# A Q projection that comes out transposed, rotated along partitions, and raw weights loaded in place

## What is computed

```python
def apply_rope(x):                       # x: b, t, heads, 128
    phase = tile(pos[:, None] * inv_freq[None, :], (1, 2))
    return x * cos(phase) + rotate_half(x) * sin(phase)    # rotate_half: (-x2, x1)

q = apply_rope((layernorm(x) @ Wq).reshape(b, t, 32, 128))
k = apply_rope((ctx @ Wk).reshape(b, t, 8, 128));  v = (ctx @ Wv).reshape(b, t, 8, 128)
logits  = 30 * tanh(q k^T * 0.0884 / 30)               # 4 query heads share one of 8 K/V heads
weights = softmax(where(mask, logits, -1e30))
x = x + tanh(g_xattn) * (weights @ v).reshape(b, t, 4096) @ Wo
h = silu(layernorm(x) @ Wg) * (layernorm(x) @ Wu)      # Wg, Wu, Wd: 4-bit, dequantised, 512 x 1376
x = x + tanh(g_ffn) * (h @ Wd).astype(float16)
```

## Time and profile before

| | |
|---|---|
| median of three runs | 811.78 us |
| the profiled execution | 811.05 us, span 809.3 us |
| TensorE busy | 772.4 us, 95% of the span |
| VectorE, GpSimd, ScalarE busy | 616.4, 494.1, 352.7 us |
| mean granted TensorE clock | 0.982 |
| slots 8 to 60 | 9.12 us each, 100% TensorE |

### The profile page before, as it was taken

The page is one execution under the profiler, slowest core; times in us unless marked ns, Lnnn a source line. Parts: engine busy times, 40 slices in busy tenths (PEclk is TensorE's granted clock), DMA queues, the critical chain, the costliest instruction groups (busy, mean ns, idle before and its releaser), DMA issues.

```text
span 809.3 us, 12403 instructions
## 1 busy us (share of the span) xinstructions
PE 772.4 (95%) x3905; PEld 644.7 (80%) x3905; DVE 616.4 (76%) x1290; ACT 352.7 (44%) x715; POOL 494.1 (61%) x391
## 2 busy tenths in 40 slices
PE   4799999999999999999999999999998689999998
PEld 3677888888888888888888888888876468888786
DVE  6798887788878887788878887786897587787531
ACT  3545443444345443444444443444443345555520
POOL 3689766566656666566665666567885466666400
PEclk9989999999999999999999999999999799999999
DMA  8410402010210201020111102020010134342011
GB/s 294 130 53 1 131 1 79 1 53 0 80 52 1 79 1 53 1 79 1 53 38 41 53 2 62 18 47 1 21 42 1 42 72 114 98 107 49 0 66 39
DMA packets 56995, 41.61 MB, mean 51 GB/s; under 512 B 22922, under 2 KB 44298, under 8 KB 56938
## 3 DMA queue, kind: packets, MB, share of 16 engines
q1 hardware_dynamic: 56938, 40.90, 17.3%
HBM read 38.77 MB, written 2.11 MB: 51 GB/s over the span
## 4 chain that ended last, share of the span: by engine, by line
PE 89%; DVE 6%; POOL 3%; issue 2%; ACT 1%; DMA 0%; DVEq 0%; ACTq 0%; POOLq 0%
PE ps_o L53 7%; PE ps_o L55 7%; PE ps_o L54 7%; PE bank_q L55 7%; PE bank_q L53 7%; PE bank_q L54 7%; PE ps_qT L1131 4%; PE bank_kv L54 3%; PE bank_kv L55 3%; PE bank_kv L53 3%; PE ps_pv L53 3%; PE ps_s L54 3%; PE ps_s L53 3%; PE ps_s L55 3%; PE ps_pv L54 2%; PE ps_pv L55 2%
## 5 line engine op out<-in xcount | busy, mean ns | idle before, releaser
L511 POOL TENSOR_TENSOR aT_lo<-attn,aT_hi 128x512 fp32r<-128x512 f32 x64 | 96.8, 1512 | 157.8 <-ACT aT_hi L679 157.8
L53 PE MATMUL bank_q<-wq_hi,xT_hi 128*128 128x512 f32 x256 | 108.4, 424 | 1.6 <-DVE wq_lo L807 1.6
L638 ACT CAST qT_hi<-ps_qT 128x512 fp32r<-128x512 f32 x64 | 37.5, 586 | 162.1 <-PE bank_kv L1132 88.7
L55 PE MATMUL bank_q<-wq_hi,xT_lo 128*128 128x512 f32 x256 | 102.8, 401 | 0.0
L54 PE MATMUL bank_q<-wq_lo,xT_hi 128*128 128x512 f32 x256 | 102.7, 401 | 0.0
L53 PE MATMUL ps_o<-wo_hi,aT_hi 128*128 128x512 f32 x256 | 101.0, 394 | 1.2 <-POOL acc L490 0.7
L54 PE MATMUL ps_o<-wo_lo,aT_hi 128*128 128x512 f32 x256 | 100.1, 391 | 0.0
L55 PE MATMUL ps_o<-wo_hi,aT_lo 128*128 128x512 f32 x256 | 100.1, 391 | 0.0
L524 POOL TENSOR_TENSOR roped<-q_cos,q_sin 128x512 f32<-128x512 f32 x61 | 79.1, 1296 | 12.2 <-DVE q_sin L833 12.2
L496 POOL TENSOR_TENSOR probs<-probs,keepT 128x512 f32<-128x512 f32 x64 | 83.7, 1308 | 3.0 <-ACT probs L655 2.9
L988 DVE SCALAR_TENSOR_TENSOR acc<-ps_o,tgates,acc 128x512 f32<-128x512 f32 x54 | 40.5, 751 | 54.5 <-PE ps_o L55 54.5
(11 more groups left out here) (220 smaller groups left out, 2218.1 us busy)
## 6 DMA issues: line engine op xcount, KB each, us to landing
wo_raw<-in_Wo SPq DMA_DIRECT2D x8, 1024.0 KB, 5.3
wq_raw<-in_Wq SPq DMA_DIRECT2D x7, 1024.0 KB, 5.8
packed<-in_gate_q SPq DMA_DIRECT2D x40, 64.0 KB, 2.2
packed<-in_up_q SPq DMA_DIRECT2D x40, 64.0 KB, 2.3
packed<-in_down_q SPq DMA_DIRECT2D x10, 256.0 KB, 3.3
acc<-in_x SPq DMA_DIRECT2D x8, 256.0 KB, 8.4
cT_raw<-in_ctx SPq DMA_DIRECT2D x8, 256.0 KB, 8.5
wkv_raw<-in_Wk SPq DMA_DIRECT2D x8, 256.0 KB, 5.9
```

What stands on the lines that cost most here:

```text
L53: nc.tensor.matmul(out, w_hi, m_hi, start=first, stop=False)
L55: return nc.tensor.matmul(out, w_lo, m_hi, start=False, stop=last)
L511: nc.gpsimd.tensor_tensor(aT_lo[:], attn[:], aT_hi[:].bitcast(F32), ALU.subtract).then_inc(a_split, 1)
L638: nc.scalar.copy(qT_hi[:], ps_qT[:])
```

## The change

Q is no longer made by sequence and then transposed. A "Q job" n makes one query head for four sequences: stationary are 128 columns of Wq, moving are four sequences of x transposed, so it comes out with the head's channels on partitions and tokens along the row. Each slot still makes one job, but four slots ahead (job s+4 in slot s); four jobs are made before slot 0, and the last four slots have none. The jobs alternate between two banks, and `ps_qT` and the four transposes of each slot go.

The rotation's halves now lie on different partitions. VectorE multiplies with the cosine (table transposed, times `live` of the tokens, which is transposed by TensorE too). ScalarE copies the two halves crosswise from PSUM to `q_sin`, 64 partitions each. GpSimd multiplies `q_sin` by the sine in place, waits for it, and adds into `q_rot`, which holds two times four jobs. `qT_hi` and `qT_lo` are made from `q_rot`, in SBUF, where before they were made from PSUM.

The raw weights are loaded into the place of the rounded ones' partner: `wq_raw[par]` lies over `wq_hi[par]`, and so on, and they are rounded in place. A load of head g waits until the last product of head g-2 that reads the buffer. K/V weights are split in two parts of 128x512 instead of four of 128x256, and the parts are handed out anew over the slots (`parts_of`); GpSimd takes the rest of a part one slot after ScalarE has rounded it, and slots 6 and 7 of each head have two parts.

At the start all x are normalised before slot 0, `xT_lo` moves from GpSimd to VectorE and reads PSUM (the copy `xn` <- `ps_x` on ScalarE goes), and `cT_lo` of sequences 2 to 7 moves from GpSimd to VectorE. The order of the first loads follows this. Tiles of the feed-forward lie at other addresses. The slots are written with plain numbers, where before three rounds of 16 were counted from a base.

```diff
+        def has_q_job(s):
+            return s + AHEAD < SLOTS
+        def q_job(n):
+            return n // B, n % B // HALF, n % HALF
 # SP
+                def load_wq(g):
+                    wait(sp, q_done, (g - 1) * B)
+                    sp.dma_start(wq_raw[g % 2][:], wq_v[:, :, g * GC:(g + 1) * GC]).then_inc(ld_wq[g % 2], 16)
+                def load_wo(g):
+                    wait(sp, o_done, (g - 1) * B)
+                    sp.dma_start(wo_raw[g % 2][:], wo_v[:, g * HG:(g + 1) * HG, :]).then_inc(ld_wo[g % 2], 16)
 # GpSimd
+                def rope(n):
+                    g, half, h = q_job(n)
+                    pool.wait_ge(q_turned, n + 1)
+                    nc.gpsimd.tensor_tensor(q_sin[:], q_sin[:], q_tab[:, 1, :].unsqueeze(1).to_broadcast([P, HALF, T]),
+                                            ALU.mult).then_inc(q_sined, 1)
+                    pool.wait_ge(q_sined, n + 1)
+                    pool.wait_ge(q_cosed, n + 1)
+                    wait(pool, qk_split, n - h - AHEAD)
+                    nc.gpsimd.tensor_tensor(q_rot[:, half, h, :, :], q_cos[:], q_sin[:], ALU.add).then_inc(q_roped, 1)
+                for b in range(2):
+                    invert_std(b)
+                split_w("wq", 0, 0)
                 invert_std(2)
+                split_w("wq", 0, 1)
+                invert_std(3)
+                split_w("wq", 0, 2)
+                split_w("wq", 0, 3)
...
+                for n in range(1, AHEAD):
+                    rope(n)
 # in slot: parts of s - 1, aT_lo, then
-                    if s >= DVE_ADDS and runs(s):
-                        wait(pool, q_mul, j + 1)
-                        wait(pool, tr_done, j)
-                        nc.gpsimd.tensor_tensor(roped[:, 0:HG, :], q_cos[:], q_sin[:], ALU.add).then_inc(q_roped, 1)
+                    if has_q_job(s):
+                        rope(s + AHEAD)
                     if runs(s - 1) and s != SLOTS:
-                        apply_mask(j - 1, s - 1)
+                        apply_mask(s - 1)
 # ScalarE
+                def turn_q(n):
+                    act.wait_ge(q_cosed, n + 1)
+                    wait(act, q_roped, n)
+                    nc.scalar.copy(q_sin[0:D // 2], q_banks[n % 2][D // 2:D])
+                    nc.scalar.copy(q_sin[D // 2:D], q_banks[n % 2][0:D // 2]).then_inc(q_turned, 1)
+                def round_q(s):
+                    act.wait_ge(q_roped, (s // HALF + 1) * HALF)
+                    wait(act, s_done, s)
+                    nc.scalar.copy(qT_hi[:], q_rot[:, s % B // HALF, :, s % HALF, :]).then_inc(q_rounded, 1)
 # in slot: round_q, round_k, round_p, aT_hi, parts, then
+                    if has_q_job(s):
+                        turn_q(s + AHEAD)
                     if runs(s):
...
                         nc.scalar.copy(v_hi[:, s % 4, :], kv_bank(s)[:, 1, :]).then_inc(v_rounded, 1)
 # VectorE
+                def cos_q(n):
+                    dve.wait_ge(q_done, n + 1)
+                    wait(dve, q_roped, n)
+                    nc.vector.tensor_tensor(q_cos[:], q_banks[n % 2], q_tab[:, 0, :].unsqueeze(1).to_broadcast([P, HALF, T]),
+                                            ALU.mult).then_inc(q_cosed, 1)
-                    nc.vector.tensor_tensor(qT_lo[:], ps_qT[:], qT_hi[:].bitcast(F32), ALU.subtract)
+                    nc.vector.tensor_tensor(qT_lo[:], q_rot[:, s % B // HALF, :, s % HALF, :], qT_hi[:].bitcast(F32), ALU.subtract)
+                    dve.wait_ge(k_rounded, s + 1)
                     nc.vector.tensor_tensor(kT_lo[:], kv_bank(s)[:, 2, :], kT_hi[:].bitcast(F32),
                                             ALU.subtract).then_inc(qk_split, 1)
 # in slot, after the partial sums of s - 2
+                    if has_q_job(s):
+                        cos_q(s + AHEAD)
+                    if s + 2 < B:
+                        ctx_rest(s + 2)
-                        rope_products(ps_q, q_cos[:], q_sin[:], q_tab, q_mul)
 # TensorE
-                    for h in range(HG):
-                        nc.tensor.transpose(ps_qT[:, h * T:(h + 1) * T], roped[:, h, :], ident[:])
+                def make_q(n):
+                    g, half, h = q_job(n)
+                    par, seqs, cols = g % 2, slice(half * HALF, (half + 1) * HALF), slice(h * D, (h + 1) * D)
+                    if n % HALF == 0 and g == 0:
+                        pe.wait_ge(x_lo, (half + 1) * HALF)
+                    wait(pe, q_turned, n - 1)
+                    for k in range(KT):
+                        mm = split_matmul(nc, q_banks[n % 2], wq_hi[par][:, k, cols], wq_lo[par][:, k, cols],
+                                          xT_hi[:, seqs, k, :], xT_lo[:, seqs, k, :], k == 0, k == KT - 1)
+                    mm.then_inc(q_done, 1)
+                for n in range(AHEAD):
+                    make_q(n)
+                    prep(AHEAD + n)
+                    if runs(s - 1) and s != SLOTS:
+                        transpose_k(s - 1)
+                    if 0 < s and has_q_job(s):
+                        make_q(s + AHEAD)
```

More of the change, by code:

```diff
@@ L26 @@
 SLOTS = KV * B
-LOOPED = 16
 INTER = 1376
@@ L42 @@
 TAIL = SLOTS - B
+AHEAD = HALF
 def wait(eng, s, n):
@@ L138, in flamingo_block @@
         attn = sb("attn", [P, GC], F32)
-        place_weights(1)
+        place_weights()
         small_at = at[0]
         probs = sb("probs", [P, 2, GC], F32)
-        roped = sb("roped", [P, HG + 1, D], F32)
-        qT_hi = sb("qT_hi", [P, GC], F32R)
-        qT_lo = sb("qT_lo", [P, GC], F32R)
+        q_rot = sb("q_rot", [P, 2, HG, HALF, T], F32)
+        k_rot = sb("k_rot", [P, D], F32)
+        qT_hi = sb("qT_hi", [P, HG, T], F32R)
+        qT_lo = sb("qT_lo", [P, HG, T], F32R)
         kT_hi = sb("kT_hi", [P, T], F32R)
@@ L343, in _ @@
                 sp.dma_start(zero_words[0:ZERO_ROWS_DOWN, 2, :], down_z.rearrange("m (j w) -> (m j) w", w=PACK)).then_inc(ld_words, 16)
-                load_wqkv(1)
+                load_ctx(4)
+                load_wkv(1)
+                for b in range(5, B):
+                    load_ctx(b)
+                load_wo(1)
                 sp.wait_ge(zero_step, 3)
@@ L350, in _ @@
                              zero_bytes[0:ZERO_ROWS_DOWN, 2, :]).then_inc(zero_stored, 16)
-                load_wo(1)
-                with sp.Fori(2, KV) as g:
-                    load_wqkv(g)
+                for g in range(2, KV):
+                    load_wq(g)
+                    load_wkv(g)
                     load_wo(g)
@@ L497, in apply_mask, with slot @@
                                             ALU.mult).then_inc(masked, 1)
-                def slot(base, group, s):
-                    j = base + s
+                def slot(s):
                     if s == SLOTS:
@@ L507, in slot @@
                     if s == SLOTS:
-                        apply_mask(s - 1, s - 1)
+                        apply_mask(s - 1)
+                    for kind, g, part in parts_of(s - 1):
+                        split_w(kind, g, part)
                     if runs(s - 3):
-                        wait(pool, a_rounded, j - 2)
+                        pool.wait_ge(a_rounded, s - 2)
                         nc.gpsimd.tensor_tensor(aT_lo[:], attn[:], aT_hi[:].bitcast(F32),
@@ L681, in slot @@
                         scale_share(s)
-                    if s < B:
-                        for head, part in early_parts[s]:
-                            round_w(head, part, head)
-                    if s >= B and runs(s + B):
-                        round_w(group + s // B + 1, s % B, (s // B + 1) % 2)
-                    if s == 0:
-                        prep(1)
+                    for kind, g, part in parts_of(s):
+                        round_w(kind, g, part)
+                    if s + 2 < B:
+                        prep_ctx(s + 2)
+                    if has_q_job(s):
+                        turn_q(s + AHEAD)
                     if runs(s):
-                        wait(act, kv_done, j + 1)
-                        wait(act, pv_done, j - 3)
+                        act.wait_ge(kv_done, s + 1)
+                        wait(act, pv_done, s - 3)
                         nc.scalar.copy(v_hi[:, s % 4, :], kv_bank(s)[:, 1, :]).then_inc(v_rounded, 1)
-                    if s + 2 < B:
-                        prep(s + 2)
                     if runs(s - 1) and s != SLOTS:
-                        cap_and_exp(j - 1, s - 1)
+                        cap_and_exp(s - 1)
                     if s == SLOTS:
-                        round_p(s - 1, s - 1)
+                        round_p(s - 1)
                     if s == TAIL + 9:
@@ new lines, in make_kv @@
+                def make_kv(s):
+                    g, b = s // B, s % B
+                    if s < B:
+                        pe.wait_ge(ctx_lo[b], 1)
+                    if b == 0:
+                        pe.wait_ge(wkv_split, (g + 1) * 2)
+                    wait(pe, qk_split, s - 1)
+                    if s == TAIL + AHEAD + 1:
```

(6 more changed lines are left out.)

558 lines of the change are left out of this document (271 added, 287 removed).

## The result

The changed kernel takes 865.44 us (median of four runs, 863.22 to 866.75), the kernel before 811.76 (810.87 to 812.43) beside it: a ratio of 1.0659, with an interval of 1.0631 to 1.0688. It is slower, as forecast, but by 54 us and not by 37, and lies above the range.

What follows compares the result with a forecast made beforehand. TensorE bounded the old kernel; after the change a ring through VectorE, ScalarE and GpSimd with collisions would, at 9.5 us a slot. 811.05 + 18 (loop) + 20 (start) - 1 (end) = 848 us; own range 836 to 860, 8-in-10 range 806 to 860.

Steps and rivals of the forecast that it cites:

- TensorE's relief: Each loop slot: four of five transposes go, 0.43 us less TensorE work, 9.12 to 8.69 us, worth 27.5 us if nothing else binds.
- what costs nothing: Whole kernel: loads into place and written-out slots cost nothing; fewer, longer K/V weight rests save GpSimd about 0.3 us a group.
- The ring and the collision: Steady loop: cosine-to-cosine dependency, with VectorE and GpSimd shutting each other out, sets 9.5 us a slot; slots 8 to 55 +18 us.
- The forecast's marks: Loop: cosines 9.5 us apart, `qT_lo` about 1.0, `p_lo` about 1.6, TensorE waiting about 0.8 a slot and some 90% busy.
- GpSimd's wait for itself: Each Q job: GpSimd waits for its own result between sine product and addition, taken as 0.21 us.
- the ring over `v_hi`: Loop: cosine, two copies, `v_hi`, `v_lo` and VectorE's work to the next cosine, 8.2 us without collisions, under TensorE's 8.69.
- The turning copies: Each Q job on ScalarE: two 64-partition copies, each taken as long as a full one, 0.59 us, next instruction 0.49 later.
- The start: Up to the eighth K transpose: 116 us against 95.9, +20 us, bounds +16 and +25; first K transpose at 50.
- The tail: Slots 56 to 63: together -1 us against 73.4 us before, bounds -7 without collisions and +4.
- so I take them as long as today: Last four slots, without Q job: 5.9 us of TensorE work, but four GpSimd instructions of 1.3 us, so length unchanged.
- can run at 8.69 (-2): Slots 56 to 59, with `p_lo` and accumulation on GpSimd: run at TensorE's 8.69 us a slot, -2 us.
- TensorE's clock drops in the new gaps: 10 us a slot: Rival: ScalarE queue waits or a lower TensorE clock; 42 us in the loop, 22 in the start, 874 us; chance 0.07.

Runs made afterwards that it cites:

- 4.7 us on the whole kernel by its experiment: Changed kernel with VectorE's three `unpack_zeros` instructions moved from slot 2 to behind the fourth cosine: 860.8 us, ratio 1.06.
- the fill: Changed kernel with six needless TensorE products ahead of the scores and six ahead of the row sums in slots 60 to 63: 861.0 us, ratio 1.0608.
- 7.6 us by its experiment: Changed kernel with ScalarE's `qT_hi` rounding put ahead of the scaled share of the output in slots 60 to 63: 858.6 us, ratio 1.0567.
- together with the addition: Kernel with four earlier edits together (819.7 us), plus Q's rotation addition moved from GpSimd to VectorE and feed-forward unpacking behind slot 60's row sums: 816.1 us.

## Why the prediction was right in the loop and wrong at both ends

**TensorE's relief**, 0.43 us a slot: right. Without collisions 37 of 48 slots take 8.69 us. The eleven with two weight rests take 9.13: the new order of the parts, which I had put among what costs nothing, costs 4.8 us in the loop as soon as the rests wait for `p_lo`.

**The ring and the collision:** right in mechanism and nearly in size, 9.40 against 9.5 us a slot. The forecast's marks stand: cosines 9.4 apart, `qT_lo` 0.94 and `p_lo` 1.57 us (about 1.0 and 1.6), TensorE busy 95% of the loop where I said some 90, and waiting for `partial` 0.45 us a slot instead of 0.8. The term most off is GpSimd's wait for itself, taken as 0.21 from the earlier trace rows: product and addition start 1.38 apart, so it is 0.08. What I missed is that the ring over `v_hi`, which I had at 8.2 without collisions, becomes as long as GpSimd's once the collisions are put into it too. +13.6 instead of +18.

**The turning copies:** 0.58 us each for 64 partitions, as a full one; the choice between the bounds was right. The second starts 0.59 behind the first, where I had 0.49. This error and that of GpSimd's own wait (0.13) have opposite signs, so a part of the closeness of 9.40 to 9.5 is luck.

**The start:** +20 forecast, +28.2 measured, above its bound of +25. The step that failed is "Seven slots of 9.5 put the eighth at 116". The slots were 9.0, 9.4, 15.4, 9.0, 9.4, 9.4 and 9.5: one of them took 6 us more. I had counted as colliding what the change touched, and not what already stood in the way of the busier GpSimd: `unpack_zeros`, 0.9 us in all with GpSimd quiet, takes 3.7 in slot 2 (4.7 us on the whole kernel by its experiment), and three weight rests meet there (the gap fell from 14.5 to 10.2 us when one of them and the wait went, with K's place changed too). The first K transpose came at 53.0, not 50: the four jobs took 25.6 us from first to fifth cosine instead of 22.4, as x batches 5 to 7 stand between their links at three places; put behind, they bring the fifth cosine 5.3 us earlier.

**The tail:** -1 forecast, +11.0 measured, outside its bounds of -7 and +4. The step that failed is "so I take them as long as today", said of slots 60 to 63: they took 47.7 us instead of 36.9. It counted instructions, and left out three things. The Q job that goes from slots 60 to 63 was the work behind which TensorE's waits for `kT_lo` and the row sums lay hidden; bare, they are 1.4 and 1.7 to 2.3 us in slots 61 to 63, and behind them the clock is at its lower level (4.0 to 5.9 us by the fill; that the missing job bares them is argued from the order of the work). `qT_hi` stood needlessly behind the share on ScalarE, though its source is no longer the slot's own transposes but lies ready in SBUF (7.6 us by its experiment; it overlaps with the clock's share, as the clock rose there too). And in slot 60 the unpacking instructions of VectorE, as old as `unpack_zeros`, are held up by GpSimd together with `qT_lo`; moving them was tried only together with the addition, where the last eight slots fell from 77.7 to 73.2 us. The "can run at 8.69 (-2)" for slots 56 to 59 failed as well: they took 36.7 us, 0.2 more than before. My rival in which "TensorE's clock drops in the new gaps: 10 us a slot" had the mechanism, but in the loop, where it is not (clock 1.00).

**Loads in place, unrolled slots, the feed-forward part:** nothing, as said (+0.4 behind the 64th K transpose). The raw weights lie over `wq_lo[par]` and not over `wq_hi[par]`, as I described it above: ScalarE rounds them into another place, and GpSimd makes the rest in place.

The Trainium skill, "SBUF — State Buffer", section "Who interferes with whom", says that VectorE in a mode that takes both ports and GpSimd exclude each other: whoever issues first gets the shared pair for the whole instruction and the other fully blocks. It adds that `copy`, `cast` and `tensor_scalar` can all enter such modes. The runs agree: the cast of 192 elements took 1.23 us beside GpSimd and 0.26 without. I had used the section for the instruction with two SBUF inputs alone, and left out that its word on a single SBUF input holds outside those modes only. The earlier trace rows had the counterexample: the normalisation has one full SBUF input and took 2.56 us; alone it takes 0.55 (changed kernel, at 14.39 us).

## What to carry to other kernels

When work moves to GpSimd, list the VectorE instructions that read and write SBUF only, the old ones too, look in the trace which of them get longer beside GpSimd, and ask for each of those whether GpSimd still has a gap there; a short one can cost nearly a whole GpSimd instruction (0.26 us became 1.23). If two engines must take turns, a wait that puts GpSimd's movable work behind VectorE's critical instruction can be worth more than less work: 31.5 us against 0.5 for taking out a whole product of GpSimd's. Such a wait also holds back what stands behind the movable work: where two rests stood ahead of `aT_lo`, the slot took 0.44 us more than TensorE's work. And work that is run ahead is missing at the other end: ask which waits it covered there.
